# A gated delta-rule layer with an FP4 feed-forward: P @ u in another loop order, the gate projection and two feed-forward units at other places, and inverse roots and gating on GpSimd

## The reference, cut to what matters

```
xn  = layernorm(x)
q,k,v = silu(causal_conv4(xn @ W));  gate = xn @ Wg
S   = S * exp(g_t);  delta = (v_t - k_t S) * beta_t
S   = S + k_t (x) delta;  o_t = q_t S          # 4096 steps, in order
attn = (rms(o) * silu(gate)) @ Wo
h   = silu(xn @ Wgate) * (xn @ Wup)            # FP4 weights, 1408 wide
y   = h @ Wdown;  out = x + attn + y / rms(y)
```

## Time and profile before

| | |
|---|---|
| median of three runs | 3537.54 us (3535.69 to 3541.82) |
| the profiled execution, its own time | 3540.35 us |
| its span | 3538.5 us |
| busy share of the span: PE, DVE, ACT, POOL | 95%, 70%, 53%, 39% |
| mean granted TensorE clock | 0.957 of 2.4 GHz |

### The profile page before, as it was taken

One profiled execution on the slowest core, in us unless ns is written; L12 is line 12 of the kernel. 1 busy time (PEld: TensorE's weight loads), 2 busy tenths in 40 slices (PEclk: granted clock), 3 DMA queues, 4 the chain that ended last, 5 costly groups with the idle time before them and its releaser, 6 DMA issues. The chain is left out here.

```text
span 3538.5 us, 118298 instructions
## 1 busy us (share of the span) xinstructions
PE 3357.7 (95%) x45632; PEld 2458.6 (69%) x45632; DVE 2465.2 (70%) x5664; ACT 1868.2 (53%) x3662; POOL 1382.3 (39%) x2321
## 2 busy tenths in 40 slices
PE   4999999999999999999999999999999999999997
PEld 3776776776777767777767777777777677677675
DVE  6777766777667767667767667776677676676763
ACT  4554555554554545554545545545545455555453
POOL 3444333443234443334443344442344432344422
PEclk8999999999999999999999999999999999999997
DMA  3111111111111111111111111101111101111111
GB/s 114 29 43 33 27 41 35 40 43 25 35 39 33 43 33 27 41 39 36 43 32 28 41 31 43 43 23 37 41 32 43 42 18 41 36 39 43 29 26 28
DMA packets 318317, 132.08 MB, mean 37 GB/s; under 512 B 277088, under 2 KB 278880, under 8 KB 317792
## 3 DMA queue, kind: packets, MB, share of 16 engines
q1 hardware_dynamic: 313824, 119.26, 13.1%
q10 hardware_dynamic: 4096, 6.42, 0.5%
HBM read 75.30 MB, written 50.33 MB: 36 GB/s over the span
## 5 line engine op out<-in xcount | busy, mean ns | idle before, releaser
L827 DVE SCALAR_TENSOR_TENSOR arena<-PS,sc,arena 128x256 f32<-128x256 f32 x2112 | 990.7, 481 | 149.3 <-ACT arena L543 50.1
L1112 PE MATMUL PS<-xh,wgu 128*128 128x256 f32 x2816 | 847.8, 338 | 4.3 <-DVE arena L827 1.5
L1113 PE MATMUL PS<-xl,wgu 128*128 128x256 f32 x2816 | 686.7, 281 | 0.0
L1125 PE MATMUL PS<-wdn,inner 128*128 128x512 f32 x1408 | 656.4, 592 | 0.0
L543 ACT ACTIVATE arena<-PS,sc 128x256 f32<-128x256 f32 x704 | 336.1, 477 | 551.6 <-PE PS L1113 537.7
L1112 PEld LDWEIGHTS PS<-xh,wgu 128*128 128x128 f32 x2816 | 530.7, 188 | 107.3 <-issue 85.9
L472 POOL TENSOR_TENSOR work<-arena 128x31 f32<-128x31 f32 (+15 forms) x992 | 509.8, 514 | 237.5 <-DMA arena<-scr_a 162.3
L1113 PEld LDWEIGHTS PS<-xl,wgu 128*128 128x128 f32 x2816 | 530.7, 188 | 90.9 <-issue 90.9
L476 POOL TENSOR_TENSOR arena<-arena,work 128x31 f32<-128x31 f32 (+15 forms) x992 | 552.1, 557 | 77.7
L1085 PE MATMUL PS<-xnT,wqkv 128*128 128x256 f32 x2048 | 512.1, 397 | 16.0 <-ACT inner L523 12.3
L1085 PEld LDWEIGHTS PS<-xnT,wqkv 128*128 128x128 f32 x2048 | 382.5, 194 | 99.1 <-ACT inner L523 28.4
(11 more groups left out here) (144 smaller groups left out, 4487.4 us busy)
## 6 DMA issues: line engine op xcount, KB each, us to landing
xt<-in_x SPq DMA_DIRECT2D x64, 256.0 KB, 2.8
scr_a<-arena SPq DMA_DIRECT2D x64, 256.0 KB, 2.1
arena<-scr_a SPq DMA_DIRECT2D x256, 64.0 KB, 3.2
obuf<-in_x SPq DMA_DIRECT2D x64, 256.0 KB, 2.8
scr_t<-arena SPq DMA_DIRECT2D x32, 512.0 KB, 2.8
arena<-scr_t SPq DMA_DIRECT2D x256, 64.0 KB, 2.3
out<-obuf SPq DMA_DIRECT2D x64, 256.0 KB, 2.0
wqkv<-in_wqkv ACTq DMA_DIRECT2D x1, 2048.0 KB, 13.2
```

The source lines that it names most:

```text
L827: eng.scalar_tensor_tensor(out=fa[:, u % 4, :], in0=PS[:, bank(u, k // 2), k % 2 * NB * P:][:, 0:NB * P], scalar=sc[:, u % 2, KB * m + k:K ...
L1112: eng.matmul(o, w, xh[:, k, :], start=True, stop=False)
L1113: ins = eng.matmul(o, w, xl[:, k, :], start=False, stop=True)
L1125: ins = eng.matmul(PS[:, b, :], inner[:, m, b * P:(b + 1) * P], wdn[:, m, :], start=(m == 0), stop=(m == FM - 1))
```

## The change

`p_times_u` is called four times, but a call is now eight heads of one batch, and the four chunks in turn for each head. All four calls stand behind the last chunk of the recurrence, with units 0, 1 and 2 after the second, third and fourth; units 3 and 4 stand behind the grams. The eight matmul groups of `gate` go into chunks 1 to 3, `project(6)` ahead of the transposes of Y, `log_decay` into chunks 0 and 1. `turn_kbq` becomes `turn_kb` and `turn_q`. Downs start after unit 7, and `turn_o` and `to_wo` stand after units 8, 10, 12, 14 and 16. Units 1 and 3 have PSUM banks 6 and 7.

POOL gets the inverse roots as a power of -0.5, the two products that make the keys of R and of the state, and the gating and scaling of o; DVE and ACT lose them, and POOL loses one copy. ACT copies the gate out of PSUM and applies Silu later. On DVE the apply of layer norm moves ahead of the units, and units 0 to 2 ahead of the first `gram_products`. On SP the first reads of `scr_a` also wait for both grams.

```diff
         def bank(u, fill):
 
-            return (2 if u % 2 and u > U_PAIRED else 4) + fill
-
-        def unit_before(u):
-
-            return u - 1 if u <= U_PAIRED else u - 2
+            return (6 if u in (1, 3) else 2 if u % 2 else 4) + fill
+
+        def proj_bank(m):
+            return 5 - m % 2 if m < 6 else m - 2
...
                     hold(eng, *a_done.at(n, b + 1))
                     eng.dma_start(scr_a[b].rearrange("c j h i -> (c j) (h i)"), kbq[:, b, :]).then_inc(a_written.sem, 16)
                     hold(eng, *a_written.at(n, 16 * (b + 1)))
+                    if b == 0:
+                        hold(eng, *gram_out.at(n, NB))
...
+        def keys_for_R(eng, t, n):
+            eng.wait_ge(*coef_done.at(n, 6))
+            eng.wait_ge(*qk_kept.at(n, NB))
             if t:
-                hold(eng, *o_gated.at(t, NB))
-            eng.tensor_copy(gs[:, :, :], gsn[:, :, :]).then_inc(gs_moved.sem, 1)
+                eng.wait_ge(*x_out.at(t, 1))
+            for b in range(NB):
+                put(eng, R[:, b, :, DV:], rows(b)[:, H:, :], ckg[:, b, :]).then_inc(rk_done.sem, 1)
+
+        def keys_for_state(eng, t, n):
+            if t:
+                eng.wait_ge(*ku_out.at(t, NC))
+            for b in range(NB):
+                put(eng, kt[:, b, :].rearrange("p (h d) -> p h d", d=DK), rows(b)[:, H:, :],
+                    ckt[:, b, :]).then_inc(kt_done.sem, 1)
...
+        def feed_forward_scale(eng, n):
+            hold(eng, *ysq_done.at(n, NB))
+            eng.tensor_scalar(yr[:, :], ys[:, :], 1.0 / C, 1e-6, ALU.mult, ALU.add).then_inc(yr_done.sem, 1)
+            hold(eng, *yr_done.at(n, 1))
+            eng.tensor_tensor(yr[:, :], yr[:, :], mhalf[:, 0, 0:NB], ALU.pow).then_inc(yr_done.sem, 1)
...
+        def gated_and_scaled(eng, t):
+            for b in range(NB):
+                eng.wait_ge(*osq_done.at(t, b + 1))
+                eng.wait_ge(*gs_done.at(t, 1))
+                eng.tensor_tensor(sq[:, b, :], sq[:, b, :], gs[:, b, :], ALU.mult).then_inc(o_gated.sem, 1)
+            hold(eng, *so_done.at(t, NB))
+            eng.tensor_scalar(ro[:, :, :], so[:, :, :], 1.0 / DV, float(np.finfo(np.float32).eps), ALU.mult,
+                              ALU.add).then_inc(ro_done.sem, 1)
+            hold(eng, *ro_done.at(t, 1))
+            eng.tensor_tensor(ro[:, :, :], ro[:, :, :], mhalf[:, :, :], ALU.pow).then_inc(ro_done.sem, 1)
+            for b in range(NB):
+                eng.wait_ge(*ro_done.at(t, 2))
+                eng.wait_ge(*o_gated.at(t, b + 1))
+                oh = sq[:, b, :].rearrange("p (h v) -> p h v", v=DV)
+                eng.tensor_tensor(oh, oh, bc(ro[:, b, :], DV), ALU.mult).then_inc(o_scaled.sem, 1)
...
         def pool_step(eng, t, n, more):
             if n:
                 split_x(eng, n)
                 expanded_g(eng, t, n)
                 masked_g(eng, t, n)
+                keys_for_R(eng, t, n)
+                if more:
+                    layer_norm_scale(eng, n.next())
                 next_tile(eng, t, n)
+                keys_for_state(eng, t, n)
+            if t:
+                gated_and_scaled(eng, t)
+            if n:
                 solve(eng, n)
+                feed_forward_scale(eng, n)
...
-            def gate_silu(b):
+                eng.activation(sqk[:, b, :], PS[:, 6 + b, :], ACT.Square).then_inc(qksq_done.sem, 1)
+
+            def gate_copy(b):
                 if not n:
                     return
                 eng.wait_ge(*gate_out.at(n, b + 1))
-                if t and b == 0:
-                    eng.wait_ge(*gs_moved.at(t, 1))
-                eng.activation(gsn[:, b, :], PS[:, 5 - b, :], ACT.Silu).then_inc(gs_done.sem, 1)
+                eng.activation(gsn[:, b, :], PS[:, 4 + b, :], ACT.Copy).then_inc(gate_copied.sem, 1)
...
@@ -652,6 +712,7 @@
             qk_squares(0)
             y_rows()
             qk_squares(1)
+            project(6)
             y_columns()
...
-            project(6)
+            project(7)
+            decay(0)
             u_rows(1)
-            project(7)
+            decay(1)
             u_rows(2)
-            decay(0)
+            masked_keys(0)
             u_rows(3)
-            decay(1)
-            if n:
-                masked_keys(0)
...
+            other_keys()
+            gate_copy(0)
+            gate_copy(1)
+            masked_keys(1)
+
+
+            queries()
+            unit(0)
+            unit(1)
             if t:
                 eng.wait_ge(*pu_out.at(t, 1))
                 for b in range(NB):
                     eng.activation(by_pair(sq[:, b, :]), paired(1, b), ACT.Copy).then_inc(o_copied.sem, 1)
...
+            unit(2)
             if t:
                 for b in range(NB):
                     eng.wait_ge(*o_copied.at(t, b + 1))
                     eng.activation(osq[:, b, :], sq[:, b, :], ACT.Square).then_inc(osq_done.sem, 1)
...
+            unit(3)
             eng.preload_act_table_set(SILU)
             if n:
-                gate_silu(0)
-                gate_silu(1)
+                gate(0)
                 eng.wait_ge(*taps_done.at(n, NQKV))
                 eng.activation(qkv[:, 4:NQKV, :], qkv[:, 4:NQKV, :], ACT.Silu).then_inc(silu_done.sem, 1)
-            if t:
...
+                unit(4)
+                gate(1)
+                unit(5)
+                if t:
+                    eng.wait_ge(*o_gated.at(t, NB))
+                eng.wait_ge(*gate_copied.at(n, NB))
+                eng.activation(gs[:, :, :], gsn[:, :, :], ACT.Silu).then_inc(gs_done.sem, 1)
+                gate(2)
             if not n:
+                o_columns()
                 return
...
-            for m in range(FM):
-                if m:
-                    unit(2 * m)
+            for m in range(3, FM):
+                unit(2 * m)
                 unit(2 * m + 1)
                 gate(m)
+                if m == 4:
+                    o_columns()
...
-            eng.preload_act_table_set(LOG)
...
-            eng.wait_ge(*ysq_done.at(n, NB))
-            eng.activation(yr[:, :], ys[:, :], ACT.Ln, bias=eps[:, 0:1], scale=1.0 / C).then_inc(yr_done.sem, 1)
-            eng.wait_ge(*yr_done.at(n, 1))
-            eng.activation(yr[:, :], yr[:, :], ACT.Exp, scale=-0.5).then_inc(yr_done.sem, 1)
...
@@ -988,48 +1009,42 @@
             products(0)
             state(1)
             products(1)
+            state(2)
             if n and more:
                 layer_norm_stats(eng, n.next())
-            state(2)
+            state(3)
+            if n and more:
+                layer_norm_apply(eng, n.next())
             conv(6)
             if n:
                 eng.tensor_copy(halo[:, :, :, :], cin[:, :, :, P:]).then_inc(halo_out.sem, 1)
...
+            unit(0)
+            unit(1)
+            unit(2)
+            gram_products(0)
             if t:
                 for b in range(NB):
                     eng.wait_ge(*osq_done.at(t, b + 1))
                     eng.tensor_reduce(so[:, b, :], osq[:, b, :].rearrange("p (h v) -> p h v", v=DV), AX.X,
                                       ALU.add).then_inc(so_done.sem, 1)
-                eng.wait_ge(*gs_moved.at(t, 1))
...
             gram_products(1)
-            if n and more:
-                layer_norm_apply(eng, n.next())
+            unit(3)
+            hidden(0)
+            hidden(1)
...
-            for m in range(FM):
+            for m in range(2, FM):
                 unit(2 * m)
                 unit(2 * m + 1)
                 hidden(m)
-                if t and m in (3, 8):
-                    result(m // 8)
+                if t and m in (6, 8):
+                    result((m - 6) // 2)
...
-                if not n:
-                    return
-                if m >= 2:
-                    eng.wait_ge(*cin_done.at(n, m - 1))
-                if m == 7:
...
+                if part != 1:
+                    if m >= 2:
+                        eng.wait_ge(*cin_done.at(n, 6 if m == 6 else m - 1))
+                for kb in range(KB) if part is None else (2 * part, 2 * part + 1):
...
-                elif u == U_PAIRED + 1:
+                elif u == 1:
+                    if fill == 0:
+                        eng.wait_ge(*knq_copied.at(n, 2 * NB))
+                        eng.wait_ge(*q_copied.at(n, 1))
+                elif u == 5:
                     if fill == 0:
                         eng.wait_ge(*p_done.at(n, NB))
                 else:
-                    eng.wait_ge(*(fa_done if fill else fa_second).at(n, unit_before(u) + 1))
+                    eng.wait_ge(*(fa_done if fill else fa_second).at(n, u - 1))
...
                     hold(eng, *kt_done.at(t, NB))
+                    if n:
+                        hold(eng, *qk_kept.at(n, NB))
...
-            def p_times_u(c):
+            def p_times_u(q):
+
                 if not t:
                     return
-                s = slice(c * CH, (c + 1) * CH)
-                hold(eng, *qs_out.at(t, c + 1))
```

(98 more changed lines are left out.)

198 lines of the change are left out of this document (76 added, 122 removed).

## The result

The changed kernel takes 3392.8 us (median of four runs, 3388.24 to 3392.96), the one before 3537.6 beside it: a ratio of 0.9586, 95% interval 0.9569 to 0.9603. The forecast was 3397, in a range of 3305 to 3480. It is read as the distance between GpSimd's casts of xh in the second tile (137.58) and the last (3223.15), over 30: 102.85 us, against 107.69 before.

A forecast was written before the change was run, and what follows sets the result against it. PE, busy 95% of the span, was taken to set the time. The terms took a step from 107.7 to 103.3 us, -136 over 31 steps, 3540.4 to 3404; the forecast was put at 3397, range 3305 to 3480.

The forecast's parts named there:

- P @ u: PE's four parts of P @ u, going round the four chunks, fall from 10.1 to 3.2 us: -6.9 a step.
- The pause: Of the 1.93 us "issue" pause in the first `p_times_u`, +0.5 us a step comes back; bounds 0 and 1.9.
- Clock: PE keeps 2.4 GHz through the recurrence in most tiles: -2.4 us a step.
- the bound of -2.9: Far bound of the clock term: the 2.9 us that the mean tile loses to the lower clock.
- Waits in the chunks: PE's wait for the state and small waits around Y and the second gram go: -1.3 us a step.
- u_rows and single gates: In the chunks, `u_rows(1)` behind ACT's work +0.4, eight gate matmuls between small ones +0.4 us a step.
- After G: Behind the last gate (G), PE stalls for DVE and ACT around grams and units: +4.6 us a step, bounds 2.5 and 7.
- POOL and the solve: The solve's round takes 101.1 to 102.9 us, PE alone 102.4 to 103: a draw, costing +0.3 a step.
- the prediction's own three marks against itself: Wrong if the power exceeds 2 us, PE waits for `scr_t` reads in every tile, or the clock falls in new stalls.
- The power: POOL's inverse roots take 0.5 us each, bounds 0.24 and 1.2, hidden by other work: cost 0.
- the solve's round sets the period: Rival: slower DMA in most tiles and solve steps lengthened by DVE, period 104.8 to 107.3, 3448 to 3525; chance 0.23.
- shorter waits: Rival: DVE catches up sooner after G and the clock never falls, period 99.5 to 101.8, 3283 to 3354; chance 0.2.

The follow-up runs named there:

- e1: Changed kernel with each part of P @ u one chunk again, old inner loop at the new places: 3555.1 us, ratio 1.0074 to the kernel before.
- e7: Kernel before with only the new order of P @ u, parts 0 to 2 behind the fourth chunk: 3474.5 us, ratio 0.9851.
- e4: Changed kernel with all eight gate pieces behind the fourth chunk, none inside the chunks: 3554.8 us, ratio 1.0058 to the kernel before.
- e14: Changed kernel with units 0 to 4 behind both grams on PE, ACT and DVE: 3516.0 us, ratio 0.9959 to the kernel before.
- e12: Kernel of e8 with the layer norm's apply on DVE moved behind the grams: 3365.6 us, ratio 0.9535 to the kernel before.
- e5: Changed kernel with both writes of A issued ahead of the reads on SP: 3363.2 us, ratio 0.9532 to the kernel before.
- e8: Kernel of e5 with GpSimd's memsets of the solve's identity also ahead of the gating: 3358.6 us, ratio 0.9506 to the kernel before.
- e2: Changed kernel with one more GpSimd power over 32 columns, ahead of the real one: 3524.3 us, ratio 0.9986 to the kernel before.
- e11: Changed kernel with one more GpSimd power over 32 columns, behind the scaling of o: 3531.4 us, ratio 0.9979 to the kernel before.
- e16: Kernel of e8 with GpSimd's product xl held until DVE's halo copy is done: 3370.1 us, ratio 0.9501 to the kernel before.

## Why the prediction was right, point by point

- *P @ u, -6.9: right in kind, too small.* The four parts take 3.56 us in the step shown, 0.44 of it pauses, against 3.24 taken. By the lines, busy time and pauses went from 368 to 120 us, 8.0 a step: the mean tile's parts had cost 11.9, not the 10.1 of the tile I took. Some of that 1.8 is time at the lower clock, which the prediction books under the clock. e1 shows that the overlap makes it.
- *The pause, +0.5: 1.2 came back* (36.7 us over 31), 0.4 of them in the parts, the others in the state's products. Instructions move in as many packets as before (383, 6.28 MB). The Trainium skill (Runtime: NRT & Kernel Launch, Instruction fetch mechanics) calls the crossing of a block mostly hidden. That "issue" is a fetch was not tried; but e7 pauses 1.73 us in the midst of 192 small products in a row, and e1, with the same products at 2.21 us a part, has 0.1 us of it in its parts in all.
- *Clock, -2.4: all of it came back*, the case of the bound of -2.9: 1.00 in the thirty steps. No run isolates its price; `log_decay` alone gained 35 us, 1.1 a step. In e4 and e14, with the same work in another order and more idle time among the small products, it is 0.96 again.
- *Waits in the chunks, -1.3:* the state's went from 31.5 to 1.1 us, -1.0.
- *u_rows and single gates, +0.8:* gates' busy time went from 247.3 to 264.0 us, +0.5 a step.
- *After G, +4.6: about right in size, by another cause in part.* Unit 8's first row starts at G+21.0, and the prediction's list adds up to about that. PE is idle for 2.7 us of the stretch; the units between small products take 1.14 us each (1417.20 to 1418.35 after part 1) and not 0.95. I had blamed the apply and conv on DVE, besides ACT's order. DVE in fact waits for ACT's first product at units 0 to 2, and e12 takes the apply away for nothing. It is the row PE, ACT, DVE through the units, 2.15 us each: ACT copies q's transposes ahead of unit 0, waits for PE at unit 1, and copies o ahead of unit 2. DVE after:

```profile
1418.57 1.59 DVE L874 SCALAR_TENSOR_TENSOR arena<-PS,sc,arena 128x256 f32<-128x256 f32 x3 [0.57 <-ACT arena L594]
1420.74 1.59 DVE L874 SCALAR_TENSOR_TENSOR arena<-PS,sc,arena 128x256 f32<-128x256 f32 x3 [0.58 <-ACT arena L594]
1422.88 1.59 DVE L874 SCALAR_TENSOR_TENSOR arena<-PS,sc,arena 128x256 f32<-128x256 f32 x3 [0.55 <-ACT arena L594]
```

- *POOL and the solve, "a draw" that costs +0.3: it decides.* The round is 11.7 + 20.8 to G, 13.3 to A's signal, 9.95 to the first solve step, 37.7 of solve, 9.4 to the product with T: 102.85, at the upper end of the 101.1 to 102.9 worked out. A's signal came 0.65 later, SP's order cost 9.95 for 9.2. PE's own list needs 101.8 (e5, e8), not 102.4 to 103, so the excess is 1.0 and not 0.3. PE waiting for the `scr_t` reads in every tile, one of the prediction's own three marks against itself, did occur; the time held because PE's list was 0.6 to 1.2 shorter than forecast.
- *The power, 0.5: the step that was wrong.* Over 32 columns 5.44 us (L520), over 2 columns 0.72 (L503, L509). (5.44 - 0.72) / 30 = 0.157 us a column, if the cost goes by the column, as two sizes suggest; my bounds (0.24 and 1.2, from products) did not hold it. A power over 2 us was the second of the prediction's marks against itself. It cost nothing by luck: o's root had 4.9 us of cover in the forecast, and the first solve step came at G+23.25 and not at G+21.9 for reasons of its own (A's signal and SP's order), so that 1.1 was left behind 5.44. With that gone a second one costs 3.9 (e2) and 4.5 (e11), as 5.44 - 1.1 says.
- *Overlooked:* the root of y stands behind the solve, and xl beside the halo's copy (+2.0 on DVE). Neither costs while the solve ends in time; both are seen in e11.
- *The total:* 3392.8 for 3397, closer than its terms, of which the parts, PE's own list and the round are each off by 0.6 to 1.2 us a step and in opposite directions. That it came out within 5 us is in part luck.

The rival "the solve's round sets the period" had the right mechanism at a price below its own bounds (104.8 to 107.3); "shorter waits" would have needed a shorter round.

## What to carry to other kernels

Put 32-row products in an order that goes round the quarters of the array, and set large matmuls between runs of them. Taking the first back costs 5.2 us a step here (e1) and taking the second back 4.9 (e4), but the order alone gave 2.1 (e7) and all but the order gave nothing (e1 against before). When work moves to an engine that carries a long dependent chain, list all that stands behind the chain in its queue. And when two chains are forecast within 1 us of each other, look at once for what is cheap on both: one reordered DMA issue was worth 0.9 us a step.

## What the runs showed of the hardware that I had not expected

- GpSimd's power took 0.72 us over 2 columns of 128 rows and 5.44 over 32, 0.157 a column between them, where a product of 31 columns takes 0.24 us in all.
- A DVE copy of 48 columns takes 2.17 us beside GpSimd's 2.35 us product and 0.21 without (e16). The Trainium skill (SBUF — State Buffer, SBUF: two separate sides) has the two engines share one pair of ports as an exclusive lock, for such copies too; the trace agrees, the copy ends as xl does. DVE's products of two SBUF operands show it as well: 0.84 us beside GpSimd's keys, 0.42 without.
- A short pause can come before a long loss of the clock: in e4 1.2 us of idle time within 1.9 were followed by 12.6 us at a mean of 0.59. In the changed kernel 0.67 us of idle time with gate matmuls behind it was followed by none.
